# Attention features in two halves around the second half of the values, and two GpSimd subtractions moved

## The chip, the cores and the metric

The kernel runs on one core of a Trainium2 chip. A core has five engines that run their own instruction streams and meet through semaphores: PE (TensorE, matrix products), DVE (VectorE), ACT (ScalarE), POOL (GpSimd) and SP (SyncE, here the issuer of all DMAs). The metric is the device time of one execution in microseconds (us), the median of several runs.

## What is computed

The reference takes `x` (128 sequences, 32 steps, 256 features) and a condition of 128 x 256, and runs four stages one behind the other:

```python
# 1. GRU over 32 steps, started from cond, fed with x
r = sigmoid(i_r + h_r); z = sigmoid(i_z + h_z); n = tanh(i_n + r * h_n)
h_new = (1.0 - z) * n + z * h
...
# 2. attention over the 32 steps of each sequence, 4 groups of 64 features, input: the GRU's states
scores = jnp.einsum('bdsh,bdth->bdst', q, k) / SCALE
weights = jax.nn.softmax(scores, axis=-1)
feats = jnp.einsum('bdst,bdth->bdsh', weights, v)
...
return feats @ Wo + bo            # x = x + this
# 3. 32 Runge-Kutta steps of a coupled oscillator, driven by the new x
# 4. gated feed-forward with ternary weights and 8-bit activations on its output, added to x
```

The change touches stage 2 alone.

## The kernel before

Everything is written by hand, instruction by instruction, in one stream for each engine; every dependence is a `wait_ge` on a semaphore. No scheduler moves anything: the order of the text is the order of each engine, and an engine that waits holds all that is behind it.

**GRU** (0 to 209 us of the trace): 32 steps; projections of x and of q, k are filled in between.

**Attention** (209 to 294 us): the 128 sequences are cut in eight groups of 16, counted by `i`. For each group PE computes

- `scores(i)` (L388): 64 small float32 products, each issued as two passes of weight load and matmul, so 128 matmuls in the trace. They use 64x32 pieces of PE.
- `values(i, 0)` and `values(i, 1)` (L409): 12 matmuls of 128x256 each, from a high and a low part of the GRU states (`v_hi`, `v_lo`) and of the weights.
- `feats_of(i)` (L429): 64 small products, again 128 matmuls in the trace, of 32x64 pieces: softmax weights (`PT`) times values (`Vs`).
- `project(i, 0)` and `project(i, 1)` (L456): 6 matmuls of 128x512 each with the output weights' parts `wo_hi`, `wo_lo` and the features' parts `f_hi`, `f_lo`.

PE's loop, with the stages of neighbouring groups interleaved, runs in iteration i: scores(i), values(i, 0), project(i-2, 0), for i = 5, 6, 7 one `weight_sum` (L438), feats_of(i-1), values(i, 1), project(i-2, 1).

ACT in iteration i: `keep_scores(i)` (L710), `keep_values(i, 0)` (L703), the exponential (L747), for i = 4, 5, 6 `weight_abs` (L730), `keep_feats(i-1)` (L718, which makes `f_hi`), `keep_values(i, 1)` (L703), for i = 5, 6 `weight_round` (L736). In iteration 0 it also makes `wo_hi` (L755), as the last thing.

DVE in iteration i: `residual(i-3, 1)` (L990), `maximum(i)` (L959, and the subtraction L963), in iteration 1 `wo_lo = wo_s - wo_hi` (L1032), `residual(i-2, 0)`, `normal(i)` (L967, L969, L971), for i = 5, 6, 7 `weight_mean` (L995) and `weight_scale` (L1000), `turn(i)` (L977, makes `PT`), `keep_feats(i-1)` (L983, makes `f_lo`). Behind the loop stand residual(5, 1), the start values of stage 3, residual(6, 0), keep_feats(7).

POOL splits the GRU states for the values: a copy that rounds (L1269, `v_hi`) and a subtraction (L1273, `v_lo`) for each of groups 1 to 7.

PE's semaphores that matter here: values(i, 0) waits for `s_split` (POOL) and for `s_V` (ACT), feats_of waits for `s_PT` (DVE), project(i, k) waits for `s_F` (DVE's f_lo), once for each half k.

Of the kernel before, what the change touches and what calls it, by code (L numbers as in the profile page):

```python
# [14 lines left out]
T = 32  # L15
# [28 lines left out]
def build(nc, xT, condT, wih, whh, bih, bhh, wq, wk, wv, wo, bqkvo, coupT, cbias, wgT, wuT, wdT, out):  # L44
# [18 lines left out]
    with ExitStack() as ctx:  # L63
# [233 lines left out]
        def tensor(pe):  # L297
# [114 lines left out]

            def feats_of(i):
                pe.wait_ge(s_V, 2 * i + 2)
                if i == 7:
                    pe.wait_ge(s_wmean, 3)
                elif i:
                    pe.wait_ge(s_F, 2 * i)
                pe.wait_ge(s_PT, i + 1)
                for js in ((0, 2), (1, 3)) if i == 7 else ((0, 1, 2, 3),):  # L420
                    if js == (1, 3):
                        r.then_inc(s_pv7, 1)
                        pe.wait_ge(s_pv7, 1)
                    for g in range(4):
                        for kk in range(2):
                            for j in js:
                                for a in (0, 64):
                                    hd = 2 * kk + a // 64
                                    r = pe.matmul(feats[i][a:a + 64, j, (4 * kk + g) * T:(4 * kk + g + 1) * T],  # L429
                                                  Vs[i % 2][quads[j], g, hd * 64:(hd + 1) * 64],  # L430
                                                  PT[i % 2][quads[j], unit(g, hd) * T:(unit(g, hd) + 1) * T],
                                                  start=True, stop=True)
                r.then_inc(s_pv, 1)

# [24 lines left out]
            for i in range(10):  # L459
                if i == 0:  # L460
                    values(0, 0)
                if i < 8:
                    scores(i)
                if 1 <= i < 8:
                    values(i, 0)
                if i >= 2:
                    project(i - 2, 0)
                if i in (5, 6, 7):
                    weight_sum(i - 5)
                if 1 <= i < 9:  # L470
                    feats_of(i - 1)
                if i < 8:
                    values(i, 1)
                if i >= 2:
                    project(i - 2, 1)
# [183 lines left out]
        def scalar(ac):  # L659
# [79 lines left out]
            for i in range(8):  # L739
                if i == 0:  # L740
                    keep_values(0, 0)
                keep_scores(i)
                if i:
                    keep_values(i, 0)
# [3 lines left out]
                if 4 <= i < 7:  # L748
                    weight_abs(i - 4)
                if i:  # L750
                    keep_feats(i - 1)
                keep_values(i, 1)
                if i == 0:
                    ac.wait_ge(ld_wo, 16)
                    ac.activation(raw(wo_hi), wo_s, ACT.Copy).then_inc(s_wo, 1)  # L755
                if i in (5, 6):
# [116 lines left out]
        def vector(ve):  # L873
# [152 lines left out]
            for i in range(8):  # L1026
                if i >= 3:
                    residual(i - 3, 1)
                maximum(i)
                if i == 1:  # L1030
                    ve.wait_ge(s_wo, 1)
                    ve.tensor_tensor(raw(wo_lo), wo_s, wo_hi, ALU.subtract).then_inc(s_wo, 1)  # L1032
                if i >= 2:
                    residual(i - 2, 0)
                normal(i)
                if i >= 5:
                    weight_mean(i - 5)
                    weight_scale(i - 5)
# [197 lines left out]
        def gpsimd(po_):  # L1236
# [26 lines left out]
            for i in range(9):  # L1263
                if i < 7:
# [5 lines left out]
                    if i == 0:  # L1270
                        po_.wait_ge(s_bulk, number[last[-1]] + 1)
                    po_.wait_ge(s_vhi, i + 1)
                    po_.tensor_tensor(raw(lo), src, hi, ALU.subtract).then_inc(s_split, 1)  # L1273
                if i == 8:
                    po_.wait_ge(ld_p[0], 112)
# [89 lines left out]
```

## Time and profile before

| what | value |
|---|---|
| median of 3 runs | 597.53 us (597.52 to 598.51) |
| the profiled execution | 599.46 us, of which the span of the trace is 597.7 us |
| mean granted TensorE clock in it | 0.994 of full speed |
| PE busy | 573.4 us, 96% of the span |
| DVE, ACT, POOL busy | 485.6, 387.9, 252.0 us |
| chain that ended last | 72% PE, 16% DVE, 5% "issue", 4% ACT |

The profiled execution is one execution; its times are the ones that the rows below carry. It is 1.93 us longer than the median of the runs. In the chain, "issue" is time in which an engine waited for nothing that the profile shows. PE's time is recorded as matmuls (PE) and as weight loads (PEld); each matmul of this kernel has one weight load.

### The profile page before, as it was taken

The numbers are of one execution on the slowest core, as the hardware profiler recorded it, in microseconds if no ns is written. First come the engines' busy times: TensorE is split into PE (matmuls) and PEld (weight loads), VectorE is DVE, ScalarE is ACT, GpSimd is POOL, SyncE is SP. The second block draws the span as 40 slices with busy tenths as digits, with TensorE's granted clock in tenths as the row PEclk, the third lists the DMA queues.
The fourth block names the chain that finished last, engine by engine and source line by source line (L and its number), as shares of the span: only waits on it lengthen the run. The fifth ranks groups of instructions, "written<-read, shape, count | busy, mean of one in ns | idle before, by whom it ended". The sixth has DMA issues, their size and how long they took to land.

```text
span 597.7 us, 16878 instructions
## 1 busy us (share of the span) xinstructions
PE 573.4 (96%) x6460; PEld 522.0 (87%) x6460; DVE 485.6 (81%) x1331; ACT 387.9 (65%) x959; POOL 252.0 (42%) x399
## 2 busy tenths in 40 slices
PE   8999999999999988999988999999999999999997
PEld 8999999999999887879776888888888888888885
DVE  3777777767777767757788999999999999999996
ACT  3545454454444454556447888888888888888885
POOL 0423323333232144240254465565565565565550
PEclk9999999999999998989999999999999999999999
DMA  8500000000000000510000000000000000000001
GB/s 261 188 2 2 1 1 2 1 1 2 2 1 1 19 3 3 152 46 3 3 0 1 11 10 19 19 10 19 19 11 19 19 10 19 19 11 19 19 11 45
DMA packets 13167, 15.05 MB, mean 25 GB/s; under 512 B 1760, under 2 KB 11296, under 8 KB 13088
## 3 DMA queue, kind: packets, MB, share of 16 engines
q1 hardware_dynamic: 13088, 13.98, 7.2%
q8 instruction: 52, 0.85, 0.6%
q14 instruction: 27, 0.22, 0.1%
HBM read 9.78 MB, written 4.19 MB: 23 GB/s over the span
## 4 chain that ended last, share of the span: by engine, by line
PE 72%; DVE 16%; issue 5%; ACT 4%; POOL 1%; SPq 1%; DMA 1%; DVEq 0%; ACTq 0%
PE PS L478 21%; PE PS L325 17%; PE PS L348 13%; PE PS L409 4%; PE PS L456 4%; PE PS L537 4%; PE PS L559 4%; DVE q_s L1112 3%; DVE h_s L1098 2%; PE PS L429 2%; DVE h_s L1085 2%; DVE PS L1061 2%; DVE h_s L1091 2%; PE PS L388 2%; ACT k_s L780 2%
## 5 line engine op out<-in xcount | busy, mean ns | idle before, releaser
L478 PE MATMUL PS<-k_s,h_s 128*128 128x128 f32 x1024 | 140.1, 280 | 8.5 <-ACT k_s L780 8.3
L478 PEld LDWEIGHTS PS<-k_s,h_s 128*128 128x128 f32 x1024 | 126.1, 191 | 19.4 <-issue 13.8
L325 PE MATMUL PS<-part 128*128 128x256 f32 x900 | 115.6, 286 | 0.0
L325 PEld LDWEIGHTS PS<-part 128*128 128x128 f32 x900 | 109.8, 191 | 0.0
L780 ACT ACTIVATE k_s<-h_s 128x128 f32<-128x128 f32 x256 | 65.3, 301 | 46.9 <-DVE h_s L1091 36.7
L348 PE MATMUL PS<-big,wrk 128*128 128x128 f32 x744 | 88.4, 275 | 1.8 <-DVE big L938 1.8
L348 PEld LDWEIGHTS PS<-big,wrk 128*128 128x128 f32 x744 | 85.8, 192 | 2.4 <-DVE big L938 2.4
L1249 POOL COPY h_s<-big 128x256 f32<-128x256 f32 x32 | 21.4, 670 | 129.1 <-DVE big L938 129.1
L478 PE MATMUL PS<-h_s 128*128 128x128 f32 x384 | 61.6, 283 | 0.4 <-DVE PS L1080 0.4
L675 ACT ACTIVATE big<-big 128x256 f32<-128x256 f32 x32 | 13.3, 416 | 63.3 <-DVE big L920 63.3
L478 PEld LDWEIGHTS PS<-h_s 128*128 128x128 f32 x384 | 50.4, 191 | 3.2 <-DVE PS L1080 0.6
L1085 DVE SCALAR_TENSOR_TENSOR h_s<-PS,h_s 128x256 f32<-128x256 f32 x128 | 53.1, 414 | 0.0
L784 ACT ACTIVATE PS<-h_s 128x256 f32<-128x256 f32 x128 | 47.1, 368 | 1.1 <-DVE part L983 1.1
L1091 DVE SCALAR_TENSOR_TENSOR h_s<-PS,h_s 128x128 f32<-128x128 f32 x192 | 46.2, 282 | 1.8 <-PE PS L478 0.7
L665 ACT ACTIVATE big<-PS,bg 128x256 f32<-128x256 f32 x96 | 41.2, 467 | 6.8 <-DVE bg L877 5.8
L1112 DVE SCALAR_TENSOR_TENSOR q_s<-PS,q_s 128x416 f32<-128x416 f32 x64 | 41.0, 643 | 1.2 <-PE PS L585 1.2
L677 ACT ACTIVATE big<-big 128x256 f32<-128x256 f32 x32 | 13.4, 418 | 38.9 <-DVE big L928 38.9
L924 DVE SCALAR_TENSOR_TENSOR big<-PS,bh,big 128x128 f32<-128x128 f32 x64 | 19.5, 347 | 18.0 <-ACT big L675 18.0
L1293 POOL TENSOR_SCALAR h_s<-h_s 128x256 f32<-128x256 f32 x32 | 13.5, 423 | 43.0 <-DVE PS L1067 41.3
L838 ACT ACTIVATE q_s<-PS,q_s 128x832 f32<-128x832 f32 x31 | 29.6, 955 | 2.9
L800 ACT ACTIVATE q_s<-q_s,mag 128x832 f32<-128x832 f32 x29 | 30.9, 1067 | 0.0
L409 PE MATMUL PS<-part 128*128 128x256 f32 x192 | 28.6, 298 | 1.9 <-issue 1.8
(187 smaller groups left out, 1193.1 us busy)
## 6 DMA issues: line engine op xcount, KB each, us to landing
out<-q_s SPq DMA_DIRECT2D x32, 128.0 KB, 1.7
x_s<-in_xT SPq DMA_DIRECT2D x14, 256.0 KB, 6.1
k_s<-in_wgT SPq DMA_DIRECT2D x4, 208.0 KB, 3.1
k_s<-in_wuT SPq DMA_DIRECT2D x4, 208.0 KB, 2.6
k_s<-in_wih SPq DMA_DIRECT2D x3, 256.0 KB, 4.5
wrk<-in_whh SPq DMA_DIRECT2D x3, 256.0 KB, 5.1
h_s<-in_wdT SPq DMA_DIRECT2D x3, 256.0 KB, 3.9
x_s<-in_xT SPq DMA_DIRECT2D x4, 128.0 KB, 3.9
```

The costliest lines, as they stand in the source:

```text
L325: r = pe.matmul(p, y, x, start=i == 0, stop=i == len(passes) - 1)
L348: r = pe.matmul(PS[:, bank, m * 128:(m + 1) * 128], whh_s[:, k, (m0 + m) * 128:(m0 + m + 1) * 128], hprev[:, k, :], start=k == 0, stop=k == 1)
L409: r = pe.matmul(PS[:, 2, (g % 2) * 256:(g % 2) * 256 + 256], raw(x), raw(w), start=n == 0, stop=n == 5)
L478: return pe.matmul(cm(stage_bank(slot), m), w, x, start=False, stop=True, skip_group_check=True)
L665: ac.activation(gi[:, n % 2, m, :], bulk_bank(u), ACT.Identity, bias=bg[:, m:m + 1]).then_inc(s_gi, 1)
L780: ac.activation(cm(th[slot % 2], m), cm(src, m), ACT.Tanh, scale=(-1 if s == 3 else 1) / lam).then_inc(s_th, 1)
L784: ac.activation(sqP, src, ACT.Square, scale=math.sqrt(cube[s]) / lam).then_inc(s_sq, 1)
L800: ac.activation(hf[:, 0:NI], hN[i % 2], ACT.Identity, scale=h_at(i, 4), bias=mag[:, 0:1]).then_inc(s_hf, 1)
L838: ac.activation(by416(sg), pg, ACT.Silu, scale=q_at(i, 2)).then_inc(s_sg, 1)
L1085: ve.scalar_tensor_tensor(w_, sqP, cube[s] * own[s], src, ALU.subtract, ALU.mult).then_inc(s_w, 1)
L1091: ve.scalar_tensor_tensor(cm(dst, m), cm(stage_bank(slot), m), of_ps[slot % 4], cm(w_, m), ALU.mult, ALU.add if slot % 4 == 2 else ALU.sub ...
L1112: ve.scalar_tensor_tensor(hN[i % 2][:, at], pg[:, g], q_at(i, 3), sg[:, at], ALU.mult, ALU.mult).then_inc(s_hN, 1)
```

## The change

- PE: for groups 0 to 6 the features are computed in two calls, `feats_low` (kk = 0, 64 matmuls in the trace) ahead of values(i, 1) and `feats_high` (kk = 1, the other 64) behind it. Only the second increments `s_pv`. Group 7 is computed as before, all of it behind project(6, 0).
- ACT: keep_values(i, 1) comes ahead of keep_feats(i-1). `wo_hi` is made in iteration 0 between keep_scores(0) and the exponential.
- DVE: the subtraction that makes `wo_lo` is gone, and `weight_mean` comes ahead of `normal`.
- POOL: makes `wo_lo`, behind its first split and behind `maximum(0)` (`s_sm` 1); its second split's subtraction waits until `maximum(1)` is done (`s_sm` 2).

```diff
-            def feats_of(i):
+            def feats_of(i, kk, js=(0, 1, 2, 3)):
+                for g in range(4):
+                    for j in js:
+                        for a in (0, 64):
+                            hd = 2 * kk + a // 64
...
+            def feats_low(i):
                 pe.wait_ge(s_V, 2 * i + 2)
-                if i == 7:
-                    pe.wait_ge(s_wmean, 3)
-                elif i:
+                if i:
                     pe.wait_ge(s_F, 2 * i)
                 pe.wait_ge(s_PT, i + 1)
...
+                feats_of(i, 0)
+
+            def feats_high(i):
+                feats_of(i, 1).then_inc(s_pv, 1)
...
-                if 1 <= i < 9:
-                    feats_of(i - 1)
+                if i == 8:
+                    feats_last()
+                elif 1 <= i < 8:
+                    feats_low(i - 1)
                 if i < 8:
                     values(i, 1)
+                if 1 <= i < 8:
+                    feats_high(i - 1)
                 if i >= 2:
                     project(i - 2, 1)
...
                 keep_scores(i)
-                if i:
+                if i == 0:
+                    ac.wait_ge(ld_wo, 16)
+                    ac.activation(raw(wo_hi), wo_s, ACT.Copy).then_inc(s_wo, 1)
+                else:
                     keep_values(i, 0)
...
+                keep_values(i, 1)
                 if i:
                     keep_feats(i - 1)
-                keep_values(i, 1)
-                if i == 0:
-                    ac.wait_ge(ld_wo, 16)
-                    ac.activation(raw(wo_hi), wo_s, ACT.Copy).then_inc(s_wo, 1)
...
                 maximum(i)
-                if i == 1:
-                    ve.wait_ge(s_wo, 1)
-                    ve.tensor_tensor(raw(wo_lo), wo_s, wo_hi, ALU.subtract).then_inc(s_wo, 1)
                 if i >= 2:
                     residual(i - 2, 0)
+                if i >= 5:
+                    weight_mean(i - 5)
                 normal(i)
                 if i >= 5:
-                    weight_mean(i - 5)
                     weight_scale(i - 5)
...
+                    if i == 1:
+                        po_.wait_ge(s_sm, 2)
                     po_.wait_ge(s_vhi, i + 1)
                     po_.tensor_tensor(raw(lo), src, hi, ALU.subtract).then_inc(s_split, 1)
+                    if i == 0:
+                        po_.wait_ge(s_wo, 1)
+                        po_.wait_ge(s_sm, 1)
+                        po_.tensor_tensor(raw(wo_lo), wo_s, wo_hi, ALU.subtract).then_inc(s_wo, 1)
```

What this makes of PE's order is seen in iterations 1 and 2 of the attention. `xN` counts products of the program here; a float32 one of L388, L429 (L418 after the change) is two matmuls in the trace. Before:

```order
L388 MATMUL PS<-k_s,q_s 32x32 x64
L409 MATMUL PS<-part 128x256 x12
L429 MATMUL PS<-big 64x32 x64
L409 MATMUL PS<-part 128x256 x12
L388 MATMUL PS<-k_s,q_s 32x32 x64
L409 MATMUL PS<-part 128x256 x12
L456 MATMUL PS<-part 128x512 x6
L429 MATMUL PS<-big 64x32 x64
L409 MATMUL PS<-part 128x256 x12
L456 MATMUL PS<-part 128x512 x6
```

The same place on PE after the change:

```order
L388 MATMUL PS<-k_s,q_s 32x32 x64
L409 MATMUL PS<-part 128x256 x12
L418 MATMUL PS<-big 64x32 x32
L409 MATMUL PS<-part 128x256 x12
L418 MATMUL PS<-big 64x32 x32
L388 MATMUL PS<-k_s,q_s 32x32 x64
L409 MATMUL PS<-part 128x256 x12
L465 MATMUL PS<-part 128x512 x6
L418 MATMUL PS<-big 64x32 x32
L409 MATMUL PS<-part 128x256 x12
L418 MATMUL PS<-big 64x32 x32
L465 MATMUL PS<-part 128x512 x6
```

The features' row is cut in two, with the values' second half between them; the number of PE's instructions is the same.

ACT in iterations 6 and 7 and the end of the attention, before (L703 keeps values, L718 features, L710 scores):

```order
L747 ACTIVATE big<-big 128x512
L730 ACTIVATE h_s,wsum<-h_s 128x1792
L718 ACTIVATE part<-PS,ba 128x512 x2
L703 ACTIVATE big<-PS 128x512
L736 ACTIVATE k_s<-k_s,mag,wscale 128x1664
L710 ACTIVATE big<-PS 128x512
L703 ACTIVATE big<-PS 128x512
L747 ACTIVATE big<-big 128x512
L718 ACTIVATE part<-PS,ba 128x512 x2
L703 ACTIVATE big<-PS 128x512
L718 ACTIVATE part<-PS,ba 128x512 x2
```

ACT at the same place after the change (L716 keeps values, L731 features, L723 scores):

```order
L763 ACTIVATE big<-big 128x512
L743 ACTIVATE h_s,wsum<-h_s 128x1792
L716 ACTIVATE big<-PS 128x512
L731 ACTIVATE part<-PS,ba 128x512 x2
L749 ACTIVATE k_s<-k_s,mag,wscale 128x1664
L723 ACTIVATE big<-PS 128x512
L716 ACTIVATE big<-PS 128x512
L763 ACTIVATE big<-big 128x512
L716 ACTIVATE big<-PS 128x512
L731 ACTIVATE part<-PS,ba 128x512 x4
```

In iteration 7 the values of the second half are kept first, and the features of group 6 stand directly ahead of those of group 7.

## Rows read from the trace of the kernel before

**Rows 1.** The page's fourth part: the chain by engine.
```profile
PE 72%; DVE 16%; issue 5%; ACT 4%; POOL 1%; SPq 1%; DMA 1%; DVEq 0%; ACTq 0%
```
**Rows 2.** Stretches: busy us (x) of PE, PEld, DVE, ACT, POOL; clock, DMA, GB/s.
```profile
229.20:232.60 3.40, 3.30 (x12) 2.91 (x12) 1.42 (x1) 1.11 (x2) 0.89 (x1) 0.50 0.02 5
...
263.30:266.70 3.40, 3.40 (x13) 2.64 (x11) 1.41 (x2) 2.64 (x3) 2.06 (x2) 0.50 0.02 5
```
**Rows 3.** Timeline of PE, iterations 1 and 2: start, length, instructions, idle before.
```profile
218.08 1.03 PE L388 MATMUL PS<-k_s,q_s 64*32 64x32 f32 x97 [0.79 <-issue]
...
222.02 1.33 PE L429 MATMUL PS<-big 32*64 32x32 f32 x110 [0.86 <-issue]
...
225.47 1.24 PE L388 MATMUL PS<-k_s,q_s 64*32 64x32 f32 x122 [0.30 <-issue]
226.64 0.86 PE L409 MATMUL PS<-part 128*128 128x256 f32 x5
229.30 1.66 PE L409 MATMUL PS<-part 128*128 128x256 f32 x7 [1.81 <-issue]
```
**Rows 4.** DMA queue: packets, MB, share; whole span, then 217.2 to 221.1 us.
```profile
q8 instruction: 52, 0.85, 0.6%
...
q8 instruction: 1, 0.02, 2.2%
```
**Rows 5.** Timeline, iterations 3 and 4: PE, and DVE's f_lo and residual.
```profile
241.80 1.49 PE L429 MATMUL PS<-big 32*64 32x32 f32 x128
...
244.75 1.57 PE L456 MATMUL PS<-part 128*128 128x512 f32 x6
...
245.01 1.37 DVE L983 SCALAR_TENSOR_TENSOR part<-PS,ba,part 128x512 fp32r<-128x512 f32 x2
...
246.25 1.29 PE L388 MATMUL PS<-k_s,q_s 64*32 64x32 f32 x128
...
246.79 0.75 DVE L990 SCALAR_TENSOR_TENSOR x_s<-PS,ba,x_s 128x512 f32<-128x512 f32 x1
...
249.00 1.57 PE L456 MATMUL PS<-part 128*128 128x512 f32 x6
```
**Rows 6.** PE in narrow windows around 243 us, and the values in full.
```profile
242.83 0.46 PE L429 MATMUL PS<-big 32*64 32x32 f32 x24
243.22 0.50 PE L409 MATMUL PS<-part 128*128 128x256 f32 x2
243.22 1.69 PE L409 MATMUL PS<-part 128*128 128x256 f32 x12
```
**Rows 7.** Matmul groups, 233 to 258 us: busy us, mean ns.
```profile
L409 PE MATMUL PS<-part 128*128 128x256 f32 x72 | 10.2, 290 | 0.0
...
L429 PE MATMUL PS<-big 32*64 32x32 f32 x384 | 4.5, 225 | 0.0
```
**Rows 8.** Timeline of PE, 259 to 267 us, iteration 5.
```profile
259.32 1.47 PE L429 MATMUL PS<-big 32*64 32x32 f32 x126
262.11 0.30 PE L429 MATMUL PS<-big 32*64 32x32 f32 x2 [1.31 <-issue]
262.33 2.16 PE L409 MATMUL PS<-part 128*128 128x256 f32 x12
264.29 2.68 PE L456 MATMUL PS<-part 128*128 128x512 f32 x6
```
**Rows 9.** Timeline, 221 to 224 us: POOL's second split, DVE beside it.
```profile
221.13 2.35 POOL L1273 TENSOR_TENSOR part<-h_s,part 128x1024 fp32r<-128x1024 f32 x1
221.29 2.73 DVE L963 TENSOR_TENSOR big<-big 128x512 f32<-128x512 f32 x1
```
**Rows 10.** Timeline, 281 to 286 us: the end of the attention.
```profile
281.70 1.27 ACT L718 ACTIVATE part<-PS,ba 128x512 fp32r<-128x512 f32 x2 [1.73 <-PE PS L429]
...
283.07 2.97 PE L456 MATMUL PS<-part 128*128 128x512 f32 x12
283.28 1.37 DVE L983 SCALAR_TENSOR_TENSOR part<-PS,ba,part 128x512 fp32r<-128x512 f32 x2
```

More of the change, by code:

```diff
@@ L411, in values, with feats_last @@
                 r.then_inc(s_Vp, 1)
-            def feats_of(i):
+            def feats_of(i, kk, js=(0, 1, 2, 3)):
[3 more added lines that the diff above has]
+                            hd = 2 * kk + a // 64
+                            r = pe.matmul(feats[i][a:a + 64, j, (4 * kk + g) * T:(4 * kk + g + 1) * T],
+                                          Vs[i % 2][quads[j], g, hd * 64:(hd + 1) * 64],
+                                          PT[i % 2][quads[j], unit(g, hd) * T:(unit(g, hd) + 1) * T],
+                                          start=True, stop=True)
+                return r
+            def feats_low(i):
                 pe.wait_ge(s_V, 2 * i + 2)
-                if i == 7:
-                    pe.wait_ge(s_wmean, 3)
-                elif i:
+                if i:
                     pe.wait_ge(s_F, 2 * i)
                 pe.wait_ge(s_PT, i + 1)
[L420 to L433, printed above, removed]
+                feats_of(i, 0)
+            def feats_high(i):
+                feats_of(i, 1).then_inc(s_pv, 1)
+            def feats_last():
+                pe.wait_ge(s_V, 16)
+                pe.wait_ge(s_wmean, 3)
+                pe.wait_ge(s_PT, 8)
+                feats_of(7, 0, (0, 2))
+                feats_of(7, 1, (0, 2)).then_inc(s_pv7, 1)
+                pe.wait_ge(s_pv7, 1)
+                feats_of(7, 0, (1, 3))
+                feats_of(7, 1, (1, 3)).then_inc(s_pv, 1)
             def weight_sum(w):
```

## The prediction

> **What bounds the kernel now.** I read the chain by engine first: 72% of it is PE, and 5% is "issue", which no wait explains [rows 1]. Then the stretch that the change touches, the attention from 213 to 294 us. From 230 us on, PE's groups stand against each other there: features 241.80, project 244.75, scores 246.25, project 249.00, each starting where the one before ends [rows 5]. So what PE executes in that stretch is the bound, and a faster DVE, ACT or GpSimd can give back only what PE waits for.
>
> What PE does lose are five gaps, all "issue": 0.79, 0.86, 0.30 and 1.81 us in iterations 1 and 2 [rows 3] and 1.31 us in iteration 5 [rows 8]. They stand inside groups, where the code has no wait. Count the matmuls between their ends: 97 scores, 12 values and the 18 features ahead of the 110 make 127; 110, 12 and 6 make 128; 122 and 5 make 127 [rows 3]. Each matmul has its weight load, so a gap can stand every 254 to 256 instructions, and the missing few are the waits, which are instructions too. The instruction queue moved 52 packets of 16 KB (0.85 MB by 52), and one of them lies between each two gaps [rows 4]. From 229.30 to 262.11 PE does 7 values, 6 project, 128 features, 12 and 6; twice a whole iteration of 292; then 128, 12, 6, 2 weight sums and 126 features: 1017 matmuls, eight times 127. I read: PE's instructions come in blocks of some 127 matmuls, the next block is asked for when one is entered, and it is there 3.94, 3.45 and 3.83 us later (218.08, 222.02, 225.47, 229.30) [rows 3]. A block that PE could do faster ends in a gap. The block before the gap of iteration 5 had two weight sums and 126 features, 1.47 us, and the gap ended 2.79 us after the first of these, about 3.2 us after the block began [rows 8]. So the loop is 3.2 to 3.9 us.
>
> Behind the two longest gaps the granted clock stands at 0.50, from 229.20 to 232.60 and from 263.30 to 266.70 us, which is 1.2 instead of 2.4 GHz [rows 2]. The second one costs: values 2.16 instead of 1.69 us [rows 8, 6], project 2.68 instead of 1.57 us [rows 8, 5], together 1.6 us.
>
> **The change part by part.**
>
> Switching between small and large matmuls. The features' last matmul starts at 242.83 + 0.46 - 0.225 = 243.07, the values' first at 243.22: 0.15 us, where features follow each other in 0.01 (1.27 us by 127) [rows 5 to 7]. The values' second starts 0.21 us later (0.50 - 0.29), the last 1.40 us after the first (1.69 - 0.29), so the other ten steps are 0.12 each, and the first lost 0.09 [rows 6, 7]. Large to small: project takes 1.50 us up to the scores, 244.75 to 246.25 [rows 5], while twelve of its matmuls take 2.97 where six take 1.57, so 1.40 for six [rows 5, 10]: 0.10. One excursion to small matmuls thus costs 0.14 + 0.09 + 0.10 = 0.33 us. Each iteration had two, scores and features; it gets a third, since the features are cut. Seven iterations have it; the first lies where blocks arrive later than PE could use them and pays nothing. 6 x 0.33 = **+2.0 us**. The lower bound is nothing, if the weight loads of the second half slip in behind the values; I take the measured price, since the same neighbours paid it everywhere.
>
> The blocks. The number of instructions is unchanged, so the borders keep their distance; their contents change. Up to 229.30 the blocks hold the same kinds and all arrive late: same gaps. From there: 7 values, 6 project, 64 features, 12 values and 38 of the second half (long, no gap); then 26 features, 6 project and 96 scores. With 0.01 for a feature or score, 0.235 for a project matmul and both switches that is 0.26 + 0.23 + 1.41 + 0.10 + 0.85 = 2.8 us, where the same block held 12 values more before and took over 4. The loop is 3.2 to 3.9, so a gap of 0.4 to 1.1 us. Going on with 127 each, the border falls into a second half in iterations 2, 3, 5 and 6: four blocks of 2.8 us, which end in the scores of iterations 3, 4, 6 and 7. The old gap of iteration 5 goes: its block is now 64 features, 12 values, 50 features and the weight sums, 3.3 us. Two of these borders (iterations 3 and 6) stand right behind large matmuls, as the one did whose loop was 3.2: 0.3 us each, by 3.2 less 2.87. For the two others I take the middle of the loop, 3.6: 0.8 us each. Together 2.2 us for 1.3 before, **+0.9 us**. Bounds: all at 3.2, 1.6, so +0.3; all at 3.9, 4.4 and 0.6 in iteration 5, so +3.7.
>
> The clock. The 1.31 us gap lies among small matmuls and the dip follows it. The new gaps are shorter and have large matmuls around them, like those of 0.79 and 0.86 us, behind which there was no dip [rows 2, 3]. So I take the second dip as gone, **-1.6 us**; the first stays with its gap of 1.81.
>
> The end. In iteration 7 the features of group 6 end later by the values and an excursion: 12 x 0.12 + 0.33 = 1.8 us. ACT's L718 starts at 283.5 instead of 281.70 and ends at 284.8; DVE's L983 runs from 284.8 instead of 283.28, its halves done at 285.5 and 286.2 [rows 10]. PE's project(5, 1) starts at 283.07 + 0.33 and needs 1.40, so project(6, 0) could start at 284.8, but waits for `s_F` until 285.5. Queued behind it on PE are features(7), which all of the end hangs on. Its second half is there in time. **+0.8 us**; zero if ACT gets at the features sooner, 1.5 (the whole lateness of L983) at worst.
>
> In earlier iterations the same lateness is covered: L983 would end at 246.38 + 1.8 and residual near 248.9 [rows 5], and the next project that needs them starts at 249.00 + 0.33. That is half a microsecond; were it gone, each iteration would pay the difference.
>
> GpSimd and DVE. L963 took 2.73 us beside GpSimd's subtraction, which had started 0.16 us before it and ended 0.54 us before its end [rows 9]. These 0.54 us are about its own length, so with the subtraction held DVE has its maximum some 2 us sooner, near 221.9, and `s_split` 2 comes near 224.3 instead of 223.5. Nobody collects either: PE needs that split for values(2, 0) at 226.64, and between 218 and 229 us it waits for blocks [rows 3]. `wo_lo` on GpSimd is half of L1273's elements, an estimated 1.2 us, in GpSimd's idle time ahead of its second copy; project(0, 0) needs it behind the values of 229.30. The earlier weight_mean costs DVE no path, nor does `wo_hi`, in a gap of ACT's. All these: 0, with GpSimd as the cover; had it none, 1.2 us once.
>
> The Trainium skill speaks against my reading. "Runtime: NRT & Kernel Launch", section on instruction fetch, gives PE 128 KiB of instruction memory in blocks of 16 KiB, and calls the cost of crossing a block mostly hidden. The blocks' size agrees with the trace's 16 KB packets; by the rest no block would come late, and the 0.9 us above would be none.
>
> **The sum.** 2.0 + 0.9 - 1.6 + 0.8 = +2.1 us. Against its own execution of 599.46 us (the span of 597.7 and 1.8 around it) that is 601.6. That execution was 1.93 us above the median of the runs, 597.53, perhaps because it has a dip that the others lack; I put the difference on the median: **599.6 us**.
>
> **The rivals.**
>
> A: the second dip stays, or moves behind a new gap, or the median's runs never had it. Against it stands that the new gaps are short; for it, that the two dips cannot be counted in the median's runs, and that the new gaps stand beside small matmuls. Then 2.1 + 1.6 = +3.7: 601.2 us.
>
> B: no new gaps, the old one and its dip gone: 2.0 + 0.8 - 1.3 - 1.6 = -0.1, 597.4 us. For it: three loops are all that I have for the price, and 3.2 against 2.8 us is not much.
>
> C, faster: the gaps are no fetch. The one at 227.50 lies beside GpSimd's third split and DVE's late softmax, and what DVE gains then reaches PE. Then the 1.81 us gap goes with its dip (values 7 of 12 in 1.66 us instead of some 0.95, project 2.40 instead of 1.57: 1.5 us) and the gap of iteration 5 with its dip: 2.0 + 0.8 - 1.81 - 1.5 - 1.31 - 1.6 = -3.4, 594.1 us. It decides from the point where half of that goes. Against it: the even count of matmuls, and that the gap of 0.79 us has no GpSimd work beside it. The Trainium skill's rule above, blocks fetched ahead, is what would make this one true.
>
> That the change doesn't do what it says I leave without a chance: the order on PE and ACT is the one described.
>
> **How the numbers follow.** The forecast has 0.45 (598.5 to 600.4), A 0.25 (to 602, and beyond it with the blocks' upper bound), B and what lies between it and the forecast 0.18 (596.5 to 598.5), C 0.12. From 596.5 to 601.8 leaves out C and the far end of A, under 2 in 10. A measurement of this kernel can tell 0.2%, 1.2 us, from no change: 596.3 to 598.7 is the same. The lower edge of the forecast and most of B lie there, 0.23; faster is C and a little of B, 0.14; slower the rest, 0.63.
>
> **What would show it.** On PE's timeline: an iteration of some 9.0 instead of 8.7 us; gaps inside the scores, 127 matmuls behind a border in a second half; none in the features of iteration 5; no stretch of clock 0.50 after 233 us; project(6, 0) waiting for DVE's L983 by 0.8 us. DVE's L963 at 0.7 us with PE's gaps of iterations 1 and 2 unchanged would speak for the blocks and against C. The prediction is wrong if the small matmuls' switch is free, or if the gaps follow something else than the count.

## The result and the profile after

The changed kernel takes 599.33 us (median of 20 runs, 597.71 to 601.62), the kernel before 598.18 us (20 runs, 594.76 to 600.79). The ratio is 1.003, with a 95% interval of 1.0015 to 1.0044: slower by some 1.8 us, between 0.9 and 2.6. The profiled execution of after took 598.97 us, of which its span is 597.2; the one of before took 599.46 and is on the long side of its runs.

In these two profiled executions the first instruction that prepares the next stage on DVE starts at 294.66 us in after and 295.32 in before; from there to the end it is 302.5 and 302.3 us. What differs lies in the attention, so I read that stretch: from the start of its first values matmul to the start of its last project matmul it is 80.60 us after and 81.03 before. That after is the shorter one here, and the slower one over 20 runs, is the first thing to explain.

The chain by engine of after, which answers to [rows 1]:

```profile
PE 72%; DVE 17%; ACT 5%; issue 4%; POOL 1%; DMA 1%; SPq 0%; DVEq 0%; ACTq 0%
```

PE's share has not moved. The windows of after over the two stretches of [rows 2] (busy us of PE, PEld, DVE, ACT, POOL, then clock, DMA share, GB/s):

```profile
229.20:232.60 3.40, 3.40 (x81) 2.81 (x80) 1.34 (x2) 1.12 (x2) 0.00 (x0) 1.00 0.02 5
263.30:266.70 3.40, 2.73 (x138) 2.21 (x137) 2.07 (x3) 2.65 (x3) 1.72 (x1) 1.00 0.00 0
```

The clock stands at 1.00 in both; there is no dip in this attention, although the long gap ahead of the first stretch is still there. PE's timeline of after, iterations 1 to 4 (start, length, instructions, idle before), for [rows 3, 5 and 6]:

```profile
217.54 1.03 PE L388 MATMUL PS<-k_s,q_s 64*32 64x32 f32 x97 [0.47 <-issue]
...
220.54 0.39 PE L418 MATMUL PS<-big 32*64 32x32 f32 x18 [0.33 <-DVE big L990]
221.25 0.71 PE L418 MATMUL PS<-big 32*64 32x32 f32 x46 [0.32 <-issue]
...
224.97 1.24 PE L388 MATMUL PS<-k_s,q_s 64*32 64x32 f32 x122 [0.41 <-issue]
226.14 0.86 PE L409 MATMUL PS<-part 128*128 128x256 f32 x5
228.81 0.99 PE L409 MATMUL PS<-part 128*128 128x256 f32 x7 [1.80 <-issue]
...
237.38 0.36 PE L388 MATMUL PS<-k_s,q_s 64*32 64x32 f32 x32 [0.42 <-issue]
...
240.71 0.86 PE L418 MATMUL PS<-big 32*64 32x32 f32 x64
241.49 1.70 PE L409 MATMUL PS<-part 128*128 128x256 f32 x12
243.12 0.86 PE L418 MATMUL PS<-big 32*64 32x32 f32 x64
243.91 1.68 PE L465 MATMUL PS<-part 128*128 128x512 f32 x6
245.52 1.29 PE L388 MATMUL PS<-k_s,q_s 64*32 64x32 f32 x128
...
249.77 0.86 PE L418 MATMUL PS<-big 32*64 32x32 f32 x64
```

The gaps of iterations 1 and 2 stand ahead of the same matmuls as in [rows 3]: 97 scores, 122 scores, 7 values. The third one's features show 46 where the 110 stood, because their other 64 are behind the values now. The 0.33 us ahead of the first 18 is no such gap: there PE waits for DVE's transposed weights (L990), because it reached this place sooner than in [rows 3]. Iteration 3 has a new gap, ahead of the last 32 of its scores. From features to features an iteration takes 249.77 - 240.71 = 9.06 us. In before it is 250.50 - 241.80 = 8.70, by the features' row in [rows 5] and the next one of before:

```profile
250.50 1.49 PE L429 MATMUL PS<-big 32*64 32x32 f32 x128
```

Iterations 5 and 6, where [rows 8] had the gap and the dip, and iteration 7 with the end of the attention:

```profile
265.57 0.32 PE L388 MATMUL PS<-k_s,q_s 64*32 64x32 f32 x21 [0.67 <-issue]
...
281.53 1.27 ACT L731 ACTIVATE part<-PS,ba 128x512 fp32r<-128x512 f32 x2 [0.25 <-PE PS L418]
282.83 1.41 DVE L996 SCALAR_TENSOR_TENSOR part<-PS,ba,part 128x512 fp32r<-128x512 f32 x2 [1.44 <-ACT part L731]
283.73 1.64 PE L465 MATMUL PS<-part 128*128 128x512 f32 x6 [0.69 <-DVE part L996]
```

No gap stands in iteration 5 any more; one of 0.67 us stands in the scores of iteration 6. The last row is new in kind: project(6, 0) waits 0.69 us for DVE's `f_lo`, which in [rows 10] came in time.

GpSimd and DVE around the second split, for [rows 9]:

```profile
217.40 1.28 POOL L1290 TENSOR_TENSOR part<-wrk,part 128x512 fp32r<-128x512 f32 x1 [2.47 <-DVE big L976]
...
221.07 0.69 DVE L976 TENSOR_TENSOR big<-big 128x512 f32<-128x512 f32 x1
221.84 2.38 POOL L1286 TENSOR_TENSOR part<-h_s,part 128x1024 fp32r<-128x1024 f32 x1 [1.02 <-DVE big L976]
...
223.53 1.24 DVE L984 TENSOR_TENSOR big<-big 128x512 f32<-128x512 f32 x1
```

The subtraction of the maximum (L963 before, L976 now) takes 0.69 instead of 2.73 us. PE's long gap beside it (1.80 us) is as long as before's; of the 0.86 us, half is now the wait for DVE above and half a gap of 0.32.

### The profile page after: what moved, and what is told of

The parts are those of the page before. It is cut to its first block, busy times and chain, and to the rows that moved or that the text cites. A ratio compares the mean times of both kernels' runs of the same rounds, so it can differ in the third digit from the quotient of the medians.

```text
span 597.2 us, 16880 instructions
## 1 busy us (share of the span) xinstructions
PE 572.9 (96%) x6460; PEld 520.8 (87%) x6460; DVE 483.0 (81%) x1330; ACT 388.0 (65%) x959; POOL 253.3 (42%) x400
## 4 chain that ended last, share of the span: by engine, by line
PE 72%; DVE 17%; ACT 5%; issue 4%; POOL 1%; DMA 1%; SPq 0%; DVEq 0%; ACTq 0%
PE PS L491 21%; PE PS L325 18%; PE PS L348 13%; PE PS L409 4%; PE PS L550 4%; PE PS L572 4%; PE PS L465 4%; DVE q_s L1123 3%; PE PS L418 2%; DVE h_s L1109 2%; DVE h_s L1096 2%; DVE h_s L1102 2%; DVE PS L1072 2%; ACT k_s L793 2%; PE PS L388 2%
## 5 line engine op out<-in xcount | busy, mean ns | idle before, releaser
L325 PE MATMUL PS<-part 128*128 128x256 f32 x900 | 115.6, 286 | 0.0
L1170 DVE TENSOR_REDUCE q_s<-q_s 128x1 f32<-128x832 f32 x30 | 30.2, 1007 | 0.0
```

Source lines behind the costliest of these rows:

```text
L325: r = pe.matmul(p, y, x, start=i == 0, stop=i == len(passes) - 1)
L1170: ve.tensor_reduce(h_at(i, 0), hN[i % 2], X, ALU.max, apply_absolute_value=True).then_inc(s_mxh, 1)
```

## The experiments

To compare runs I take three numbers from the trace of each: the attention's length as above, the sum of PE's pauses in it from 0.12 us on (gaps of the kind "issue" and the waits for DVE and ACT together), and the number of dips (stretches of 3.4 us at a granted clock near 0.50). The runs without a trace say something on dips too, because the mean granted clock of each is on record: one dip makes it 0.997, two 0.994. So the table has a column of runs at 0.997 or less. The kernels other than after were run on four chips in turn, and before ran beside them each time; its median there is given for each row.

| kernel | attention, us | pauses, us | dips | runs with a dip | median, us | before beside it, us | ratio to before |
|---|---|---|---|---|---|---|---|
| before, profiled twice | 81.03, 79.17 | 5.70, 4.96 | 2, 1 | 68 of 86 | 598.18 | | 1 |
| moves only | 79.01 | 6.17 | 0 | 9 of 12 | 598.41 | 597.98 | 1.0013 (0.9997 to 1.0029) |
| after, profiled twice | 80.60, 80.75 | 5.85, 5.52 | 0, 0 | 6 of 20 | 599.33 | 598.18 | 1.003 (1.0015 to 1.0044) |
| halves only | 80.63 | 5.76 | 0 | 1 of 12 | 599.07 | 597.98 | 1.0018 (1.0002 to 1.0034) |
| after, group 6 whole | 78.35 | 4.15 | 0 | 1 of 12 | 597.59 | 597.98 | 0.9998 (0.9983 to 1.0014) |
| after, three pieces | 80.08 | 4.10 | 0 | 2 of 10 | 598.98 | 598.52 | 0.9998 (0.9983 to 1.0012) |
| after, 36 pairs ahead | 84.18 | 6.18 | 2 | 6 of 6 | 603.93 | 598.18 | 1.01 (1.0065 to 1.0134) |
| after, 96 pairs ahead | 83.79 | 7.88 | 1 | 5 of 5 | 603.92 | 598.18 | 1.0094 (1.0068 to 1.012) |
| before, 104 pairs ahead | 80.57 | 6.27 | 1 | 12 of 12 | 601.61 | 598.18 | 1.0046 (1.0025 to 1.0066) |
| before, scores beside features | 92.08 | 15.94 | 2 | 2 of 2 | 609.93 | 598.18 | 1.0192 (1.0148 to 1.0237) |
| before, group 4 cut, and the moves | 78.68 | 5.71 | 0 | 3 of 12 | 597.70 | 598.52 | 0.9974 (0.996 to 0.9989) |
| before, group 4 cut | 78.92 | 5.80 | 0 | 2 of 12 | 596.90 | 598.20 | 0.9981 (0.9968 to 0.9994) |

The 86 runs of before are those beside the other kernels. By their clock 18 of them had no dip, with a mean of 596.6 us, 55 had one (598.5), 12 two (600.1) and one three (601.2). The 14 runs of after without a dip have a mean of 598.9 us, the 6 with one 601.1. A run with one dip is thus 1.5 to 2.4 us longer than one without, on each chip and in both kernels, and at the same number of dips after is 2.3 to 2.6 us longer than before. The halves alone, without a dip, are at 598.9 us and 2.3 above the runs of before without one on the same chip; from chip to chip that mean of before goes from 596.3 to 597.1.

**The halves alone.** After, with `wo_hi`, `wo_lo`, `weight_mean` and the second split put back to where before has them:

```diff
-                    if i == 1:
-                        po_.wait_ge(s_sm, 2)
                     po_.wait_ge(s_vhi, i + 1)
```

> The features in two halves alone: PE's and ACT's new order, while wo_hi, wo_lo, weight_mean and the second split stand as before. Theory (PE and its instruction blocks bound this stretch): DVE's subtraction of iteration 1 takes 2.7 us again, PE's gap in the values of iteration 2 is 1.8 us as in both kernels, an iteration is 9.07 us, PE waits 0.7 us for f_lo ahead of project(6, 0); the time is that of the whole change, about 1 us over before. Rival (what DVE gains reaches PE): the four moved pieces are worth 1.5 to 2 us, so this is 2.5 to 3 us over before.

Measured: 599.07 us, 1.1 us above before by the medians, and 80.63 us of attention, as after. The rival, 2.5 to 3 us above before, fails. What the other parts change is seen on DVE and GpSimd alone. DVE's and GpSimd's timeline of this kernel:

```profile
221.28 2.37 POOL L1286 TENSOR_TENSOR part<-h_s,part 128x1024 fp32r<-128x1024 f32 x1
221.44 2.75 DVE L976 TENSOR_TENSOR big<-big 128x512 f32<-128x512 f32 x1
```

With the subtraction back beside it, the same DVE instruction takes 2.75 us again. In after the hold keeps the two apart, and the same instruction takes 0.69. Nothing on PE shows the 2 us.

**The moves alone.** Before, with `wo_hi` early on ACT, `wo_lo` on GpSimd, the held subtraction and the earlier `weight_mean`:

```diff
+                    if i == 1:
+                        po_.wait_ge(s_sm, 2)
                     po_.wait_ge(s_vhi, i + 1)
```

> Before, with wo_hi early, wo_lo by GpSimd, the second split held and weight_mean early; the features whole. Theory: DVE's subtraction of iteration 1 falls from 2.7 to 0.7 us and nothing collects it: PE's gaps of 0.3 to 1.8 us stand every 127 to 128 matmuls as before, the time is that of before within 0.5 us. Rival: the 1.8 us gap in the values of iteration 2 shrinks with DVE's work, 1.5 to 3 us faster than before.

Measured: 598.41 us and a ratio whose interval holds 1. PE's gaps of this kernel:

```profile
221.96 1.33 PE L429 MATMUL PS<-big 32*64 32x32 f32 x110 [0.86 <-issue]
...
228.98 0.99 PE L409 MATMUL PS<-part 128*128 128x256 f32 x7 [1.53 <-issue]
...
261.51 0.30 PE L429 MATMUL PS<-big 32*64 32x32 f32 x2 [1.88 <-issue]
```

They stand where [rows 3] and [rows 8] have them, so GpSimd and DVE have no part in them: rival C falls. The gaps are long (1.53 and 1.88 us), yet no dip follows either: this execution's mean clock is 1.00, and the twelve values behind the second gap take 1.70 us.

**The end.** After, with the features of group 6 whole again, ahead of values(7, 1), and ACT keeping them first in iteration 7:

```diff
                 feats_of(i, 0)
+                if i == 6:
+                    feats_high(6)
...
-                if 1 <= i < 8:
+                if 1 <= i < 7:
                     feats_high(i - 1)
```

> The changed kernel, but the features of group 6 whole and ahead of values(7, 1), and kept by ACT before the values. Theory: the wait of 0.69 us ahead of project(6, 0) goes, and one excursion to small matmuls (0.33 us) too: 1.0 us less than the changed kernel, about the time of before. Rival (what hangs behind is late for another reason, DVE's start values): no gain.

Measured: 597.59 us. That is 1.5 us less than the halves on the same chip, and 1.7 us less than after. The timeline of the attention's end in this kernel, PE and DVE:

```profile
280.92 2.97 PE L467 MATMUL PS<-part 128*128 128x512 f32 x12
281.12 1.37 DVE L1000 SCALAR_TENSOR_TENSOR part<-PS,ba,part 128x512 fp32r<-128x512 f32 x2
```

Twelve project matmuls in one row again, with no wait between the sixth and the seventh. That is 0.69 us, and the excursion of that group is saved, 0.36: 1.05 of the 1.5 us. For the remaining 0.4 us I have no row of its own; the other pauses of the profiled execution are 0.7 to 1.0 us shorter than in the three with halves, and whether that is chance I can't tell from one trace.

**Where the gaps fall.** If PE's instructions come in blocks counted from the program's start, then instructions added far ahead must shift every border by their number. I put pairs of waits that hold at once into steps 1 to 26 of the GRU stage ahead of the attention. A pair of `wait_ge` becomes one instruction: the trace has 575 semaphore instructions on PE with 36 pairs, and 539 in after. A matmul with its weight load is two, so 36 pairs must shift the borders by 18 matmuls. After with 36 such pairs:

```diff
                 hprev = g_h[(t - 1) % 2] if t else cond
+                for _ in range(2 * (36 // 26 + (t <= 36 % 26)) if 1 <= t < 27 else 0):
+                    pe.wait_ge(s_const, 1)
```

> The changed kernel with 36 waits on a semaphore that has long been reached, each an instruction of PE's of its own, spread over the GRU's steps 1 to 26: nothing else moves, but all later borders of 256 instructions come 36 instructions (18 matmuls) earlier in the program. Theory (blocks of 256): the gaps move by 18 matmuls: in scores of iteration 1 from 31 to 13 matmuls in, in iteration 2 from the fifth matmul of the values into the scores, some 2.5 us at 114 to 116 matmuls in, and one of about 1 us inside the values of iteration 5; about 1.5 us longer than the changed kernel. Rival (gaps belong to GpSimd or DVE): the gaps stay where they are, time unchanged.

PE's timeline of this kernel, the rows with gaps:

```profile
224.30 0.33 PE L420 MATMUL PS<-big 32*64 32x32 f32 x12 [0.28 <-issue]
...
227.76 0.28 PE L390 MATMUL PS<-k_s,q_s 64*32 64x32 f32 x12 [2.00 <-issue]
...
258.73 1.47 PE L411 MATMUL PS<-part 128*128 128x256 f32 x11 [1.44 <-issue]
...
290.59 5.79 PE L467 MATMUL PS<-part 128*128 128x512 f32 x17 [0.82 <-issue]
```

and its window over the first stretch of [rows 2]:

```profile
229.20:232.60 3.40, 3.40 (x25) 2.36 (x26) 1.05 (x3) 1.11 (x2) 0.00 (x0) 0.50 0.00 0
```

Each gap stands where the count puts it. The time is 603.93 us, 4.6 above after, much more than expected. In the attention this is accounted for: two dips came back (229.2 and 290.6 us), and 80.6 + 0.3 of gaps + 2.7 for two dips make 83.6, against 84.18. The profiled execution is 3.6 us above the one of after, all of it in the attention. The median is another 1.4 us above the profiled execution, and the clocks of the runs say why: three of the six, the profiled one among them, had two dips (0.994; 601.7, 602.5 and 603.8 us), the others more (0.989 to 0.992; 604.1, 606.3 and 607.9 us).

The instruction queue settles what the gaps are. PE's 13461 instructions are 52.6 blocks of 256, and the queue carries 52 packets of 16 KB; the traces have the time of each. In after the packets around iterations 1 and 2 start at 218.71, 222.28 and 226.55 us and have landed at 219.91, 223.59 and 227.43; the gaps end at 221.25, 224.97 and 228.81, which is 1.3 to 1.4 us behind. In the attentions of all fourteen traces PE has 91 pauses of the kind "issue", and 88 of them end 1.2 to 1.6 us behind the landing of a packet. The other three are named below. A packet takes 0.9 to 1.9 us from start to landing, and that alone lets the gap at one border differ from one execution to the next.

**Two more shifts.** After with 96 pairs, and before with 104:

```diff
-                for _ in range(2 * (36 // 26 + (t <= 36 % 26)) if 1 <= t < 27 else 0):
+                for _ in range(2 * (96 // 26 + (t <= 96 % 26)) if 1 <= t < 27 else 0):
```

> The same with 96 such waits. Theory: borders 48 matmuls earlier; the gap of 0.5 us at 31 matmuls into the scores of iteration 1 is gone and stands at 111 instead, one of some 2.3 us stands 86 matmuls into the scores of iteration 2, the gaps of 1.8 us in the values of iteration 2 and of 0.67 us in the scores of iteration 6 are gone, one of about 0.7 us stands some 100 matmuls into the scores of iteration 5; about 1.5 us shorter than the changed kernel, 3 us shorter than with 36. Rival: unchanged.

> The kernel before with 104 such waits. Theory: the gaps of 1.8 us (values of iteration 2) and 1.3 us (features of iteration 5) go; new ones of 0.8 to 1.1 us stand 107 matmuls into the scores of iteration 1, 94 into the features of group 0, 82 into the scores of iteration 2, in the values of iteration 4 and near the end of the features of group 6; about 1.2 us shorter than before, if the clock does not dip. Rival: unchanged.

Rows with gaps on PE's timeline of after with 96 pairs:

```profile
217.89 0.25 PE L390 MATMUL PS<-k_s,q_s 64*32 64x32 f32 x5 [1.78 <-issue]
229.67 0.57 PE L390 MATMUL PS<-k_s,q_s 64*32 64x32 f32 x42 [1.90 <-issue]
```

and of before with 104:

```profile
224.62 0.53 PE L431 MATMUL PS<-big 32*64 32x32 f32 x34 [2.14 <-issue]
...
247.55 0.99 PE L411 MATMUL PS<-part 128*128 128x256 f32 x7 [0.67 <-issue]
252.02 0.34 PE L431 MATMUL PS<-big 32*64 32x32 f32 x14 [0.78 <-issue]
```

The positions came out right again, with three exceptions, all with 96 pairs: I had not foreseen the gap of 1.78 us in the scores of iteration 0 nor one of 1.12 us in the values of iteration 4 (both on the count), and the one that I expected 111 matmuls into the scores of iteration 1 is not there. The times did not: I expected both kernels faster, and they are slower by 4.6 us than after and 3.4 us than before. Part is in the attention: with 96 pairs the gaps are 2.0 us more than in after, and there is a dip; another 1.0 us lies ahead of the attention and 0.6 us behind it. With 104 the attention is as long as in before; its profiled execution is only 0.6 us above that of before, and the 1.0 us behind the attention (303.38 to the end instead of 302.33) belong to it; its median lies 1.5 us above that execution. The clocks of the runs account for most of that: all five runs with 96 pairs had one dip or more and three of them at least two (0.992 to 0.994), where after has 0.3 dips per run; with 104 pairs the four runs with one dip, the profiled one among them, took 599.6 to 600.1 us, and the eight with two or three 601.5 to 603.6. What stays open is the 1.0 us ahead of the attention and the 0.6 and 1.0 us behind it. A shift of all borders is no free gift, since it moves them in the stages ahead and behind as well, and here it brought more dips.

**Small matmuls side by side.** Before, with the features of the group before right behind the scores, from iteration 3 on: 256 small matmuls in a row, so some block holds nothing else.

```diff
                     scores(i)
+                if 3 <= i < 8:
+                    feats_of(i - 1)
...
-                if 1 <= i < 9:
+                if i in (1, 2, 8):
                     feats_of(i - 1)
```

> The kernel before with features(i-1) directly behind scores(i) from iteration 3 on: one excursion to 256 small matmuls instead of two to 128. Theory of the blocks: a border falls inside each such run and the next block is done after 1.3 us, so a gap of 2.3 us in the features of iterations 3 to 7; five of them, and the old one of iteration 5 gone; five excursions of 0.33 us less: 8 us longer than before, more if the clock dips. Rival (no blocks; the switch alone counts): 1.6 us shorter than before.

PE's timeline of this kernel, iterations 3 and 4:

```profile
239.34 1.15 PE L429 MATMUL PS<-big 32*64 32x32 f32 x95
242.68 0.69 PE L429 MATMUL PS<-big 32*64 32x32 f32 x33 [2.20 <-issue]
243.30 2.93 PE L409 MATMUL PS<-part 128*128 128x256 f32 x12
...
255.44 0.96 PE L429 MATMUL PS<-big 32*64 32x32 f32 x71 [2.42 <-issue]
256.33 2.93 PE L409 MATMUL PS<-part 128*128 128x256 f32 x12
```

609.93 us (two runs), 1.0192 times before. This order has one excursion less per iteration than before has, and still loses 11.5 us: PE gets through some 127 small matmuls in about 1.3 us, and then waits 2.20 us for the next ones. The row behind each of these two gaps shows the clock: twelve values in 2.93 us instead of 1.69. Of the five gaps of 2.3 us that I expected, these two came, of the other three 0.19, 1.24 and 1.49 us. What came besides is a pause of 0.41 to 0.54 us ahead of the features in iterations 4 to 7. It stands at no border. One of the four is a wait for DVE's `f_lo`; the other three are the "issue" pauses that no packet goes with, and their cause is not shown. All pauses together are 15.9 us, 10.2 more than in before, and are most of the loss. Without them and two dips the attention is 92.1 - 15.9 - 2.7 = 73.5 us, no shorter than the whole order's 72.8, though five excursions are saved; where these went I did not settle.

The Trainium skill, "Runtime: NRT & Kernel Launch", section "Instruction fetch mechanics", says that blocks of 16 KiB, 256 instructions, are fetched in sequence, and that this is hidden because an engine dispatches slower than they arrive. The 256 agree with the spacing of the gaps above. That it is hidden does not hold here: PE waited 2.20 and 2.42 us in blocks of small matmuls alone, and up to 1.8 us in mixed ones.

**One cut more.** After, with values(i, 1) cut in two as well and the second features behind each: features, 6 values, 32 features, 6 values, 32 features.

```diff
-                if i < 8:
+                if i == 0:
                     values(i, 1)
-                if 1 <= i < 8:
-                    feats_high(i - 1)
+                elif i < 8:
+                    values(i, 1, (2,))
+                    feats_of(i - 1, 1, gs=(0, 1))
+                    values(i, 1, (3,))
+                    feats_of(i - 1, 1, gs=(2, 3)).then_inc(s_pv, 1)
```

> The changed kernel with one excursion more in each of iterations 1 to 7: the high half of the features is itself cut in two, with the last six of the values' matmuls between the pieces. Theory: an excursion costs 0.37 us of PE each time (an iteration 9.4 us where it was 9.07), 2.2 to 2.6 us in all, of which the gap in the scores of iteration 3 and part of the one in iteration 6 give back 0.5 to 1 us: 1.5 to 2 us over the changed kernel. Rival (a switch is free, and the halves' price lies in ACT or DVE): 0.

PE's timeline of this kernel, iteration 3:

```profile
240.37 0.86 PE L419 MATMUL PS<-big 32*64 32x32 f32 x64
241.16 0.98 PE L409 MATMUL PS<-part 128*128 128x256 f32 x6
242.06 0.46 PE L419 MATMUL PS<-big 32*64 32x32 f32 x32
242.45 0.97 PE L409 MATMUL PS<-part 128*128 128x256 f32 x6
243.35 0.46 PE L419 MATMUL PS<-big 32*64 32x32 f32 x32
243.75 1.67 PE L466 MATMUL PS<-part 128*128 128x512 f32 x6
...
249.60 0.86 PE L419 MATMUL PS<-big 32*64 32x32 f32 x64
```

I expected 1.5 to 2 us more than after, and there is nothing of it: 598.98 us, and 598.8 in the mean of the eight runs without a dip, for after's 598.9. An iteration is 9.23 us here, 0.17 more than in after. All of that is in the values, twice 0.90 us from start to start instead of once 1.63; the features' three pieces together are as long as the two were. Over six iterations this is 1.0 us (80.08 - 4.10 = 76.0 us without gaps, for 75.0 in the halves), and the gaps gave it back: 4.10 us instead of 5.7, since none stands in the scores of iterations 2, 3 and 6. So my price of an excursion holds for 64 features cut off, and not for one that cuts them further.

**Only where the gap was.** If the one thing worth having in the change is that the gap of iteration 5 goes, with the dip behind it, then it is enough to cut the features of group 4. Before, with that cut, with the moves and then without:

```diff
                     values(i, 1)
+                if i == 5:
+                    high(4)
```

> Features cut in halves for group 4 alone (iteration 5), the others whole, and the four moved pieces of ACT, DVE and GpSimd as in the changed kernel. Theory: the gap of 1.3 to 1.9 us in the features of iteration 5 gives way to one of some 0.7 us in the scores of iteration 6, for one excursion of 0.37 us: 0.3 to 0.9 us less than before, which these runs can hardly tell from nothing; 1.5 to 2 us less than the changed kernel. Rival (gaps do not depend on the order): 0.4 over before.

> The kernel before with the features in halves for group 4 alone and nothing else moved. Theory (the split of iteration 5 takes the gap of 1.2 to 1.9 us out of the place where small matmuls stand alone, for 0.36 us and a gap of 0.7): the same 0.2 to 0.3% under before as with the four moved pieces. Rival (the pieces on DVE and GpSimd made that gain): the time of before.

PE's timeline of the kernel with the moves, iterations 5 and 6:

```profile
260.45 0.74 PE L418 MATMUL PS<-big 32*64 32x32 f32 x50
261.59 0.34 PE L418 MATMUL PS<-big 32*64 32x32 f32 x14 [0.40 <-issue]
...
263.46 1.10 PE L388 MATMUL PS<-k_s,q_s 64*32 64x32 f32 x107
265.24 0.32 PE L388 MATMUL PS<-k_s,q_s 64*32 64x32 f32 x21 [0.67 <-issue]
```

Both are a little faster than before, with ratios of 0.9974 and 0.9981 and neither interval reaching 1, and faster than after. The moves make no difference that the two intervals could tell. The gap of 1.2 to 1.9 us is two short ones now, 1.07 and 1.15 us together, so the gaps' sum is no smaller (5.71 and 5.80 against 5.61 on average); without them the attention is 73.0 and 73.1 us, one excursion above the 72.8 of the whole order. What is won is the dips. None is in these two traces, and only 3 and 2 of the twelve runs each have one, where 20 of 23 and 15 of 17 runs of before beside them do. Among runs without a dip nothing is won: 597.1 and 596.9 us, against 597.1 and 596.8 in before (only 3 and 2 such runs).

**Before and after once more**, one profiled execution each, for the dips:

> The kernel before, one more profiled execution, for its gaps and its clock. Theory: the same six gaps, their sizes apart by some 0.3 us; whether the clock dips behind the two long ones is chance, so none, one or two dips. Rival (my prediction's): two dips again, in the same places.

> The changed kernel, one more profiled execution. Theory: the same gaps; a dip behind the one of 1.8 us may come or not. Rival (my prediction's): that dip comes, and no second one.

597.13 and 599.23 us. Before has one dip this time, behind iteration 5's gap of 1.22 us; the window of that stretch:

```profile
260.60:264.00 3.40, 3.40 (x15) 3.11 (x14) 1.41 (x2) 2.28 (x4) 1.24 (x2) 0.50 0.02 5
```

After again has none, with gaps of 1.53 us in iteration 2 and 0.95 us in iteration 6.

## Why the prediction was right, and by what

The forecast of 599.6 us stands beside 599.33, in its own range and with the sign that had the highest chance. By its steps:

**The switches, +2.0 us: right.** Take gaps and dips from the attention. The whole order leaves 72.8 us (moves only, 79.01 - 6.17, which has no dip); the halves leave 74.75, 75.2 and 74.9. That is +2.1 us. In an iteration: 9.06 instead of 8.70 us, 0.36 for one more excursion where I had 0.33. It splits as foreseen: the features take 0.78 + 0.79 instead of 1.42 us, the values between them 1.63 instead of 1.53, and the project behind the second half 1.61 instead of 1.50.

**The blocks, +0.9 us: the mechanism right, the term mis-sized.** The count of 127 held in every kernel, and the shifts moved the gaps with it. But the halves' pauses are 5.71 us on average; without the 0.69 us of the wait at the end 5.0, for 5.6 in the whole order. That is -0.6 us where I had +0.9. (The other waits among them, 0.63 us for `f_lo` ahead of the last project, which all six executions compared here have and which my list of five gaps lacks, and up to 0.4 us for DVE or ACT in iterations 1 and 2, do not change this: the "issue" gaps alone are 4.1 and 4.8 us.) The failed step is the gap given to each border in a second half. I had 0.8 us for those that end in the scores of iterations 3 and 6, and they took 0.42, 0.13 and 0.14, and 0.67, 0.95 and 0.35 in the three executions; I had 0.3 us for those of iterations 4 and 7, and there was none. At the two new gaps of after the next block was there 3.4 and 3.65 us after the block ahead of it was entered, inside my 3.2 to 3.9. Two things made the gaps smaller. These blocks ran 3.0 us (3.4 less 0.42, 3.65 less 0.67) instead of my 2.8. And the block behind was in part asked for earlier: its packet starts 0.6 to 0.7 us after the first matmul of the block in iteration 3 (four traces of halves), 0.7 to 1.3 us after it at the gap in iteration 6, and 0.9 to 1.6 us after it in iterations 1 and 2, where most of my loops were read. What sets how much earlier, and why no gap at all stands in the scores of iterations 4 and 7, I leave open. The old gap of iteration 5 went, as foreseen, but for 0.17 us in after again, and it was worth 1.2 to 1.9 us rather than 1.31.

**The clock, -1.6 us: the size about right, the account wrong in part.** Five profiled executions with the features in halves or thirds and the borders in their old place have no dip; three of the whole order have 2, 1 and 0. One dip costs about 1.35 us (79.17 - 4.96 - 72.8 = 1.4; 81.03 - 5.70 - 72.8 = 2.5 for two), so the mean is -1.3 us. But I said that the first dip stays with its gap of 1.81 us: the gap stayed, at 1.80, and the dip did not. And the moves alone have gaps of 1.53 and 1.88 us with no dip. A dip behind such a gap is a matter of chance in an execution. Eight traces are too few for the chance, but the clocks of the runs give it: 0.95 dips per run in the 86 of before, 0.3 in the 20 of after. So the change takes away 0.65 of a dip on average, at 1.35 us by the traces and 1.5 to 2.4 by the runs: 0.9 to 1.6 us. I had one dip less, from two to one. The typical run of before had one, which is why the profiled one with its two dips was long.

**The end, +0.8 us: right.** 0.69 us, on the row that I had named, and gone when group 6 was whole.

**GpSimd and DVE, 0: right**, with L976 at 0.69 us and nobody to collect it; `wo_lo` took 1.28 us for my 1.2. One thing I missed: the held subtraction now lies beside DVE's `normal`, L984, which takes 1.24 us beside it. It hides too.

**The sum.** 2.1 - 0.6 + 0.7 - 1.3 = +0.9 us, where I had +2.1. Measured is +1.15 by the medians and +1.8 by the ratio. Without the clock it is +2.2 us, and the runs with no dip say +2.3 (598.9 against 596.6). So the effect is smaller than forecast by 0.3 to 1.0 us, and the forecast hit 599.3 because its base, 597.53 from three runs, was 0.65 us below the median of 20. Right in sign and mechanism, helped in size. And the profiled execution of before, the one with two dips, explains the puzzle of the first section: it was 1.3 us longer than the median of its kernel, and after's was 0.4 shorter.

Of the rivals, C is refuted. B (no new gaps, no dip) is about as near to the traces as the forecast: it says -0.1 where they say +0.9 and the forecast +2.1, and what it lacks are new gaps of some 0.9 us. A, a dip in spite of the change, happened in 6 of after's 20 runs, though in neither of its traces, and in every run of the kernels with 36 and 96 pairs.

## What to carry over

When an engine runs very short instructions, count them: on PE here a border stands every 127 matmuls, and PE stalls there when it has done a block before the next has come, some 3 to 4 us after it entered the block. Large matmuls put into such a block shorten the stall, at 0.36 us for every further excursion to small ones. Cut only the block that stalls: one cut bought 1.1 to 1.6 us here, all of it, as far as the few runs without a dip can tell, in dips of the clock that did not come, and the same cut in seven places cost 1.8. And before a difference of 2 us is read from two profiled executions, take their gaps and dips out, and see what is left of the difference; and look at the granted clock of the other runs, which counts the dips of each.

## What I had not expected of the hardware

- The granted clock fell to 0.50 for 3.4 us behind gaps of 0.82 (with 36 pairs, at 290.6 us), 1.22, 1.31, 1.78, 1.81, 2.00, 2.20 and 2.42 us, and with 104 pairs at 287.9 us, where the last gap is one of 0.33. It did not fall behind others of 1.44, 1.53, 1.80, 1.88, 1.90 and 2.14 us. With one kernel, before, 18 of 86 runs had no dip, 55 one, 12 two and one three.
- In the attentions 88 gaps of PE end 1.2 to 1.6 us after a packet of 16 KB has landed on the instruction queue; the packet itself takes 0.9 to 1.9 us.
- The same block border behind the same matmuls ended in gaps from 0.35 to 0.95 us (scores of iteration 6 in the halves' order) and from 1.26 to 1.80 us (values of iteration 2 in that order); in before the latter took 1.81 us once and 0.81 the other time.
- Cutting six values off six others with 32 features between them cost 0.17 us, half of what cutting the features at 64 had cost; for the features themselves a further cut cost nothing.
- Seventy-two waits that hold at once, spread over 26 steps, are 36 instructions of PE and made a kernel of 600 us 4.6 us slower. Most of that is dips: two to four in each of its six runs, and 0.3 on average in after.
